# Transposed one-hots moved from the neighbour sums into the pair count, in a graph network on one Trainium2 core

## The reference

```python
x += gin(x)          # 3 rounds: agg = segment_sum(x[dst], src); two 128x128 layers; batch norm
x = layernorm(x); x += gatv2(x)      # 3 rounds of attention over the edges
x = layernorm(x); x += hypergraph(x) # d_v, sums to 625 hyperedges, sums back: segment_sum(he[he_idx], node_idx)
x = layernorm(x); x = 2 * x + messages(x); x = layernorm(x)   # an MLP over the edges, summed by dst
```

## Time and profile before

| | |
|---|---|
| median of three runs | 7289.36 us |
| the profiled execution, its own time | 7309.43 us |
| its span in the trace | 7306.3 us |
| VectorE busy | 3755.9 us (51%) |
| TensorE matmuls busy | 4516.1 us (62%) |
| ScalarE busy | 1443.0 us (20%) |
| GpSimd busy | 3988.3 us (55%) |
| mean granted TensorE clock | 0.786 of full speed |

### The profile page before, as it was taken

How to read it: one execution, slowest core, us unless ns; L and a number is a source line. 1 busy time by engine, 2 the same in 40 slices (tenths; PEclk the granted TensorE clock), 3 DMA queues, 4 the chain that set the end, 5 groups by cost and what they waited for, 6 DMA issues and landing times. The chain is left out here.

```text
span 7306.3 us, 132331 instructions
## 1 busy us (share of the span) xinstructions
PE 4516.1 (62%) x28367; PEld 3658.6 (50%) x28368; DVE 3755.9 (51%) x9359; ACT 1443.0 (20%) x2857; POOL 3988.3 (55%) x3213
## 2 busy tenths in 40 slices
PE   4887777456666663566666446666663746666664
PEld 2554433345565553455555435555553445555554
DVE  6999544544444446344444544444446344444445
ACT  0334200101111110011111201111111024444442
POOL 0000000188888844788888268888770048888883
PEclk9888899667788776788787767777886867777777
DMA  1222446146666662566666436666662511111111
GB/s 33 60 60 78 122 126 174 28 126 179 180 186 178 175 173 73 151 183 178 176 184 176 120 99 172 178 180 177 182 180 61 129 34 42 42 41 42 42 41 27
DMA packets 768883, 874.40 MB, mean 120 GB/s; under 512 B 282710, under 2 KB 548112, under 8 KB 768762
## 3 DMA queue, kind: packets, MB, share of 16 engines
q10 hardware_dynamic: 300702, 352.23, 17.0%
q1 hardware_dynamic: 212060, 307.39, 14.7%
q0 software_dynamic: 256000, 213.32, 12.8%
HBM read 626.18 MB, written 242.79 MB: 119 GB/s over the span
## 5 line engine op out<-in xcount | busy, mean ns | idle before, releaser
L483 POOL DMA_INDIRECT rows<-row_table,now x2400 | 2965.8, 1236 | 2359.5 <-issue 2313.0
L483 POOL DMA_INDIRECT rows<-node_table,now x800 | 1019.7, 1275 | 710.1 <-issue 704.6
L801 DVE SCALAR_TENSOR_TENSOR z<-zp,own 125x512 f32<-125x512 f32 x672 | 464.9, 692 | 1694.3 <-PE zp L723 809.5
L720 PE MATMUL zp<-parts,hot_t 125*125 x8100 | 764.8, 255 | 780.5 <-issue 652.0
L720 PEld LDWEIGHTS zp<-parts,hot_t 125*125 125x125 bf16 x8100 | 716.1, 163 | 861.8 <-issue 855.1
L734 PE MATMUL sums<-values,hot 125*125 125x137 f32 x5376 | 916.0, 324 | 283.3 <-issue 124.5
L734 PEld LDWEIGHTS sums<-values,hot 125*125 125x125 f32 x5376 | 879.2, 228 | 411.0 <-issue 345.6
L723 PE MATMUL zp<-rows,ident 125*125 x2700 | 956.4, 485 | 184.2 <-SPq L504 133.3
L649 ACT CAST hot<-hot 125x500 f32<-125x500 bf16 x672 | 408.7, 608 | 2467.6 <-remote 731.4
L723 PEld LDWEIGHTS zp<-rows,ident 125*125 125x125 f32 x2700 | 561.2, 231 | 280.5 <-issue 203.8
L970 PE MATMUL turn<-ident,onehot 125*126 125x125 f32 x904 | 178.9, 333 | 510.8 <-DVE onehot L538 413.4
(11 more groups left out here) (384 smaller groups left out, 5043.9 us busy)
## 6 DMA issues: line engine op xcount, KB each, us to landing
gathered<-rows SPq DMA_DIRECT2D x600, 231.0 KB
back<-gathered ACTq DMA_DIRECT2D x588, 231.0 KB
hot_t<-hots_t ACTq DMA_DIRECT2D x678, 122.1 KB
hot<-hots ACTq DMA_DIRECT2D x672, 122.1 KB
counts<-pairs SPq DMA_DIRECT2D x75, 685.1 KB
rows<-row_table,now POOLq DMA_INDIRECT x2400
hots_t<-hot_t ACTq DMA_DIRECT2D x225, 109.4 KB
hots<-hot_dst SPq DMA_DIRECT2D x224, 109.4 KB
```

Source lines behind the costliest of these rows:

```text
L483: pool.indirect_dma_start(rows[:, q, j, :], None, table, bass.IndirectOffsetOnAxis(ap=now[:, half, lane + j:lane + j + 1], axis=0)).then_i ...
L720: pe.matmul(zp[:, p, j, 0:ROW], hot_t[:, q, j * P:(j + 1) * P], own[part], start=part == 0 and j % 2 == 0, stop=False, skip_group_check=True)
L801: dve.scalar_tensor_tensor(out=z[:, p, :, :], in0=zp[:, p, :, 0:D], scalar=0.0, in1=rows_of(own_att, HALF), op0=ALU.max, op1=ALU.mult).the ...
```

## The change

The transposed one-hots are made inside the count of pairs, and no longer in the later sums:

- `slot_rows`, filled as before, is written to a DRAM table `slot_table` in tile order. From there ScalarE's queue reads the slots of two teams at a time, the same 1000 values into each of the 125 partitions (`spread_slots`, f16), one loop turn (four teams) ahead.
- VectorE compares them with the lane number, one instruction of 500 columns for each team, behind that team's eight others (`make_hot_t`). SyncE stores two teams' `hot_t` at a time in `hots_t`, and two teams' `hot_dst` at a time in `hots`.
- The loop runs over 56 groups of four teams; all one-hot buffers hold four teams.
- A cell of `hot_dst` is 126 columns wide (`CELL`) and not 125; the matmuls still read 125 of them. `hots`, the attention's `hot` and `hot32` (ScalarE widens one into the other) follow: 504 columns for 500.
- `lanes` is written by GpSimd.
- The later sums lose their matmuls into `turn`, the comparisons, the stores and their buffers.
- `prepare_runs` stores two zero rows in `hots_t` in place of one.

```diff
 GROUP = BSTEPS // 4
+CELL = P + 1
 SIXTY = 60
...
-        hot = sc.sb("hot", [P, AHEAD, HALF * P], BF16)
-        hot32 = sc.sb("hot32", [P, 2, HALF * P])
+        hot = sc.sb("hot", [P, AHEAD, HALF * CELL], BF16)
+        hot32 = sc.sb("hot32", [P, 2, HALF * CELL])
...
-                    ins = pe.matmul(sums[:, p, 0:ACCW], hot32[:, p, j * P:(j + 1) * P], values[:, p, j, :], start=j == 0, stop=j == HALF - 1)
+                    ins = pe.matmul(sums[:, p, 0:ACCW], hot32[:, p, j * CELL:j * CELL + P], values[:, p, j, :], start=j == 0, stop=j == HALF - 1)
...
 def count_pairs(nc, g, counts, loads):
 
+    QUARTERS = TEAMS // HALF
     with Scope(nc) as sc:
         nodes = sc.sb("nodes", [P, SIDE], F16)
-        lanes = sc.sb("lanes", [P, P], BF16)
-        hot = sc.sb("hot", [P, 2, HALF, SIDE], BF16)
-        hot_dst = sc.sb("hot_dst", [P, 2, HALF, P], BF16)
+        lanes = sc.sb("lanes", [P, CELL], BF16)
+        hot = sc.sb("hot", [P, HALF, HALF, SIDE], BF16)
+        hot_dst = sc.sb("hot_dst", [P, HALF, HALF, CELL], BF16)
+        slot_rows = sc.sb("slot_rows", [SIXTY, FIFTEEN, P], F16)
+        spread_slots = sc.sb("spread_slots", [P, HALF, HALF * P], F16)
+        hot_t = sc.sb("hot_t", [P, HALF, HALF * P], BF16)
         zero = sc.sb("zero", [P, CHUNK], BF16)
         warmed = sc.sb("warmed", [P, 1])
         bank = sc.ps("bank", [128, 2, 512])
         turn = sc.ps("turn", [128, 4, 512])
-        names = ("noded", "laned", "cleared", "made", "warm", "hot_made", "loaded", "turned")
-        noded, laned, cleared, made, warm, hot_made, loaded, turned = (sc.sem(x) for x in names)
-        hot_used, copied, hot_kept = (sc.sems(x) for x in ("hot_used", "copied", "hot_kept"))
+        names = ("noded", "laned", "cleared", "made", "warm", "hot_made", "loaded", "turned", "tabled", "hot_t_made")
+        noded, laned, cleared, made, warm, hot_made, loaded, turned, tabled, hot_t_made = (sc.sem(x) for x in names)
+        hot_used, copied, hot_kept, hot_t_kept, slots_in = (sc.sems(x) for x in ("hot_used", "copied", "hot_kept", "hot_t_kept", "slots_in"))
         block = sc.block()
+        flat_slots = g.slot_table.rearrange("m r e -> (m r e)")
+
+        def make_hot_t(eng, i, p):
+            if p % 2 == 0:
+                eng.wait_ge(slots_in[p // 2], landed(i, len(PIECES)))
+                eng.wait_ge(hot_t_kept[p // 2], before(i, 16 * len(PIECES)))
+            eng.tensor_scalar(hot_t[:, p, :], spread_slots[:, p, :], g.lane[:, :], None, ALU.is_equal).then_inc(hot_t_made, 1)
 
         @block.sync
         def _(sp):
             for dst, src in loads:
                 sp.dma_start(dst, src, allow_slow_non_contiguous=dst.shape[0] * dst.shape[-1] < 1000).then_inc(loaded, 16)
-            with sp.Fori(0, LOOPS) as i:
-                for p in range(2):
-                    k = 2 * i + p
-                    sp.wait_ge(made, HALF * k + HALF)
-                    wide(sp, g.hots[bass.ds(k, 1), :, :].rearrange("a p n -> (a p) n"),
-                         hot_dst[:, p, :, :].rearrange("p j n -> p (j n)"), hot_kept[p])
-            for p in range(2):
-                sp.wait_ge(hot_kept[p], before(LOOPS, 16 * len(PIECES)))
+            with sp.Fori(0, QUARTERS) as i:
+                for h in range(2):
+                    k = HALF * i + 2 * h
+                    sp.wait_ge(made, HALF * k + 2 * HALF)
+                    wide(sp, g.hots[bass.ds(k, 2), :, :].rearrange("a p n -> p a n"),
+                         hot_dst[:, 2 * h:2 * h + 2, :, :].rearrange("p a j n -> p a (j n)"), hot_kept[h])
+                    sp.wait_ge(hot_t_made, k + 2)
+                    wide(sp, g.hots_t[bass.ds(k, 2), :, :].rearrange("a p n -> p a n"), hot_t[:, 2 * h:2 * h + 2, :], hot_t_kept[h])
+            for h in range(2):
+                sp.wait_ge(hot_kept[h], before(QUARTERS, 16 * len(PIECES)))
+                sp.wait_ge(hot_t_kept[h], before(QUARTERS, 16 * len(PIECES)))
             sp.wait_ge(loaded, 16 * len(loads))
 
         @block.gpsimd
         def _(pool):
             pool.iota(nodes[:, :], pattern=[[1, SIDE]], base=0, channel_multiplier=0,
                       allow_small_or_imprecise_dtypes=True).then_inc(noded, 1)
+            pool.iota(lanes[:, :], pattern=[[1, CELL]], base=0, channel_multiplier=0,
+                      allow_small_or_imprecise_dtypes=True).then_inc(laned, 1)
 
         @block.vector
         def _(dve):
             dve.memset(zero[:, :], 0.0).then_inc(cleared, 1)
-            dve.tensor_copy(lanes[:, :], g.iota[0:P, :]).then_inc(laned, 1)
             dve.wait_ge(laned, 1)
             dve.wait_ge(noded, 1)
-            prime(dve, hot_kept)
-            with dve.Fori(0, LOOPS) as i:
-                for p in range(2):
-                    k = 2 * i + p
-                    dve.wait_ge(hot_used[1], after(k, 2))
-                    dve.wait_ge(hot_kept[p], before(i, 16 * len(PIECES)))
+            prime(dve, hot_kept, hot_t_kept)
+            with dve.Fori(0, QUARTERS) as i:
+                for p in range(HALF):
+                    k = HALF * i + p
+                    dve.wait_ge(hot_used[1], after(k, HALF))
+                    if p % 2 == 0:
+                        dve.wait_ge(hot_kept[p // 2], before(i, 16 * len(PIECES)))
                     for j in range(HALF):
                         s = bass.ds(HALF * k + j, 1)
                         dve.tensor_scalar(hot_dst[:, p, j, :], lanes[:, :], g.slot[:, s], None, ALU.is_equal).then_inc(made, 1)
                         dve.tensor_scalar(hot[:, p, j, :], nodes[:, :], g.src_lo[:, s], g.src_unit[:, s],
                                           ALU.is_equal, ALU.mult).then_inc(hot_made, 1)
+                    make_hot_t(dve, i, p)
 
         @block.tensor
         def _(pe):
@@ -1230,16 +1248,16 @@
             for m in range(FIFTEEN):
                 ins = pe.transpose(turn[0:SIXTY, m // 4, (m % 4) * P:(m % 4 + 1) * P], g.slot[:, SIXTY * m:SIXTY * (m + 1)], g.ident[0:P, 0:P])
             ins.then_inc(turned, 1)
-            with pe.Fori(0, LOOPS) as i:
-                for p in range(2):
-                    k = 2 * i + p
+            with pe.Fori(0, QUARTERS) as i:
+                for p in range(HALF):
+                    k = HALF * i + p
                     for h in range(2):
                         pe.wait_ge(copied[h], after(k, 1))
                         for j in range(HALF):
                             if h == 0:
                                 pe.wait_ge(made, HALF * k + j + 1)
                                 pe.wait_ge(hot_made, HALF * k + j + 1)
-                            ins = pe.matmul(bank[0:P, h, 0:CHUNK], hot_dst[:, p, j, :], hot[:, p, j, h * CHUNK:(h + 1) * CHUNK],
+                            ins = pe.matmul(bank[0:P, h, 0:CHUNK], hot_dst[:, p, j, 0:P], hot[:, p, j, h * CHUNK:(h + 1) * CHUNK],
                                             start=False, stop=False, skip_group_check=True)
                         ins.then_inc(hot_used[h], 1)
             for h in range(2):
@@ -1253,16 +1271,33 @@
             act.wait_ge(turned, 1)
             for m in range(0, FIFTEEN, 4):
                 n = min(4, FIFTEEN - m)
-                act.copy(g.slot_rows[:, m:m + n, :], turn[0:SIXTY, m // 4, 0:n * P].rearrange("p (m l) -> p m l", l=P)).then_inc(warm, 1)
-            with act.Fori(0, LOOPS) as i:
-                for p in range(2):
-                    k = 2 * i + p
-                    w = window_of(act, g, k)
-                    for h in range(2):
-                        act.wait_ge(hot_used[h], after(k))
-                        act.wait_ge(copied[h], after(k, 1))
-                        act.copy(counts[:, bass.ds(w, 1), h * CHUNK:(h + 1) * CHUNK].rearrange("p w n -> p (w n)"),
-                                 bank[0:P, h, 0:CHUNK]).then_inc(copied[h], 1)
+                act.copy(slot_rows[:, m:m + n, :], turn[0:SIXTY, m // 4, 0:n * P].rearrange("p (m l) -> p m l", l=P)).then_inc(warm, 1)
+            act.wait_ge(warm, 5)
+            act.dma_start(g.slot_table.rearrange("m r e -> r m e"), slot_rows[:, :, :]).then_inc(tabled, 16)
+            act.wait_ge(tabled, 16)
+
+            def load_slots(i, h):
+                wide(act, spread_slots[:, 2 * h:2 * h + 2, :].rearrange("p a n -> p (a n)"),
+                     flat_slots[bass.ds(HALF * P * (HALF * i + 2 * h), 2 * HALF * P)].partition_broadcast(P), slots_in[h])
+
+            def keep_counts(k):
+                w = window_of(act, g, k)
+                for h in range(2):
+                    act.wait_ge(hot_used[h], after(k))
+                    act.wait_ge(copied[h], after(k, 1))
+                    act.copy(counts[:, bass.ds(w, 1), h * CHUNK:(h + 1) * CHUNK].rearrange("p w n -> p (w n)"),
+                             bank[0:P, h, 0:CHUNK]).then_inc(copied[h], 1)
+
+            for h in range(2):
+                load_slots(0, h)
+            with act.Fori(0, QUARTERS - 1) as i:
+                for p in range(HALF):
+                    keep_counts(HALF * i + p)
```

(48 more changed lines are left out.)

9 lines of the change are left out of this document (removed).

## The result

The changed kernel takes 7211.35 us (median of 4 runs, 7194.60 to 7215.24) against 7290.48 us for the kernel before on the same chip (4 runs, 7284.66 to 7293.24). The ratio is 0.9888, 95% interval 0.9871 to 0.9905: 1.1% faster, some 80 us, where 148 us were forecast. The forecast of 7141.0 us and its range of 7122 to 7172 us missed; the sign was right.

The account below looks back on a forecast made before the run. VectorE was taken to pace the count of pairs. Terms -199.6 + 58.9 - 9.0 - 11.4 + 11.7 + 1.0 = -148.4 us took 7289.36 to 7141.0 us, range 7122 to 7172.

Parts of the forecast that it names:

- the slots' loads: In the count's loop, ScalarE's loads of slots are ready after 5.7 us against 6.8: hidden, costed at 0.
- Rival (c): In the count's loop, slots or stores land 0.3 us late at each of 110 halves: +33 us, 7174; 8%.
- Rival (d): Loads of slots become the count's pace, landing in 4.95 us or more: slower than before, 7350 at 5.5 us; 2%.
- later sums: The first two later sums become as short as the third without their turned rows: -199.6 us, ±5.
- `hot_t`: In the count, 224 new VectorE instructions of 350 ns, a slot of 263 ns each: +58.9 us.
- (b): In the count, hot_t runs at the f32 slope: +22.6 us, 7163; 6%.
- `CELL`: One-hot cells of 126 columns, in hot_dst and in ScalarE's widening, change nothing: 0.
- the end: At the count's end the last store waits for hot_t and stands behind hot_dst's store: +1 us.
- the waits for stores: In the count, VectorE's waits for stores of hot_dst go, as stores get two teams' time: -11.4 us.
- the loop turns: In the count, 56 fewer loop branches at 0.16 us each: -9.0 us.
- The start: At the count's start VectorE stalls for the slots' table to be stored and loaded: +11.7 us, bounds 7.8 and 20.

Follow-up runs that it names:

- e11: Changed kernel with ScalarE reading the next team's window number ahead of the two DMA issues instead of behind them; 7212.79 us, ratio 0.9828 to the kernel before.
- e7: Changed kernel with each load of slots one DMA to 125 lanes instead of two to 112 and 13; 7157.09 us, ratio 0.9817 to before.
- e12: Changed kernel with each load of slots one DMA to 125 lanes and four window numbers read at once; 7198.9 us, ratio 0.9805 to before.
- e6: Changed kernel with ScalarE reading four window numbers at once at a turn's start, loads still on its queue; 7142.18 us, ratio 0.9797 to before.
- e2: Changed kernel with the loop's loads of slots issued by SyncE's queue instead of ScalarE's; 7134.43 us, ratio 0.9767 to before.
- e10: Changed kernel with the loads of slots issued by GpSimd instead of ScalarE; 7190.73 us, ratio 0.9799 to before.
- e4: Changed kernel with the loop's loads of slots left out, so sums are not the reference's; 7134.0 us, ratio 0.9776 to before.
- e5: Kernel before with only the padding to 126 columns and lanes drawn by GpSimd; 7284.19 against 7285.78 us, ratio 0.9994.
- e9: Kernel before with one-hot buffers and loop four teams deep, stores of two teams, no slots or padding; 7314.23 us, ratio 0.9959.
- e3: Changed kernel with spread_slots holding eight teams instead of four, loads still issued by ScalarE; 7179.51 us, ratio 0.9834 to before.
- e8: Changed kernel with SyncE issuing the loads and hot_t made one turn of four teams behind; 7133.85 us, ratio 0.9786 to before.

## Why the prediction was right or wrong

**The failed step is that of the slots' loads**: "It is hidden with 1.1 us to spare, so I cost it at 0". It cost some 75 us (585.7 - 510.8), the whole miss of the count and more. The landing in the step was fair: 1.2 + 2.5 = 3.7 us from the first issue was taken, 3.34 measured. What failed was ScalarE's lag. I took the 2.0 us by which its last copy trailed VectorE in a kernel whose ScalarE issues nothing, and measured was a median of 4.16 us. Then 4.16 + 3.34 = 7.5 us (7.59, the median of the sums) stand against the 6.3 us from the end of one `hot_t` to the start of the one that needs the load. These 6.3 were 6.8 in the prediction, which counted a branch that takes no time and began at the start of the `hot_t` and not at its end. The same comparison sorts the other runs: 6.79 in e11, 6.43 in e7 and 6.29 in e12 with 23 to 28 us of waits in the loop, 6.22 in e6 with 9, 4.44 in e2 with none (e10's 5.45 is the median beside its four late ones). The sentence "What ScalarE's queue holds behind a late load is only the next team's copies" named the cause and valued it at nothing: for these copies TensorE waits, and the copies that follow carry the next issue.

**Rival (c)** has the form of what happened, slots late in the loop, but its cause (three streams in bursts) did not: e2 and e4 have the same stage at shares of 0.64 and 0.38. It priced 0.3 us at 110 halves; the stage lost 75 / 110 = 0.68 us for each. Rival (d) wanted a landing of 4.95 us; 3.34 came. Only the one piece of e7 lands so late.

**Terms that held**: later sums -199.6 (measured -199.6); `hot_t` +58.9 (224 x 0.260 us = +58.2, 348 ns for the 350 forecast), so (b) falls; `CELL` 0 (e5); no wait for stores in the changed kernel; the end +1 (now 3.94 us from `hot_t`'s end to the next stage, where 2.77 us lay behind the last `hot` before).

**Terms that were mis-sized**: the waits for stores, -11.4 forecast and -29 to -30 measured (e9), and the loop turns, -9.0 forecast and 0 measured. I had put down to the branch what the deeper buffers took away as waits for stores; that the two terms together, -20.4, come near the -30 is luck. The start, +11.7 forecast, 8.1 measured here and 9.7 to 10.2 in e2 to e4: the table was in memory and the loads issued at 152.69, 4.4 us after the store's issue, not 6.0.

With SyncE issuing the loads, where the step holds, the stage grew by 510.8 - 471.3 = 39.5 us. From the terms as measured: 58.2 + 10.2 - 30 + 1.0 (the end, 3.81 us in e2 against 2.77) = 39.4. The ratio 0.9767 is then a little better than the 0.980 of the forecast. Of the span's difference in the changed kernel, 97.6 = 199.6 - 114.4 (count) + 13.7 (the attention's chance) - 1.3.

**What stays open** is TensorE's clock. It was granted 0.64 or 0.65 of the full clock, a mixture of its levels of 1.2 and 2.4 GHz, in the changed kernel, e3 and e11, 0.72 and 0.74 in e7 and e12, and 0.80 to 0.96 in the others. A slower TensorE makes ScalarE's chain longer, and the chain's waits may be what lowers the clock; no run separates the two. A low clock alone did not hold VectorE up as far as the runs go: e2 has stretches at 0.73 (220 to 245 and 345 to 370 us) with a team every 2.216 us. Nor does the clock follow TensorE's waits for copies (14.2 us at 0.72 in e7, 26.7 at 0.81 in e8). Nor was the split between issues and register loads measured by itself: e6 and e11 show that the register loads' place and number, with what stands around them, are worth 63 and 39 us of the stage, with the issues unchanged.

## What to carry to other kernels

A DMA issue is an instruction of the queue that it stands in, and so is a register load: think twice before putting either on the queue of an engine for whose results another engine waits, and look for a queue with time to spare (here SyncE's). The lag that I read from a trace in which the queue had nothing to issue was half of the one that came, and a margin of 1.1 us over it was no margin: the next issue stands behind the copies that were delayed. The order inside such a queue is free to change, and was worth 39 us with the same instructions. And a small gap that recurs once a turn is not the branch's for that: look at where in the turn it lies, and at what landed just before it.
